# Two of four block sums of each square layer made by accumulating transfers on GpSimd's queue, with signs turned; the weights' check spread over one more tile

## The reference, cut to what matters

```
h = silu(x @ w1.T * w1_s) * (x @ w2.T * w2_s)
h = gelu(h @ h1_w.T * h1_s)          # square layer 0
h = gelu(h @ h2_w.T * h2_s)          # square layer 1
g = silu(h @ w3_w.T * w3_s)
```

## Time and profile before

| | us |
|---|---|
| median of 3 runs | 1295.23 (1295.19 to 1295.3) |
| profiled execution, its own time | 1296.77 |
| its span in the trace | 1295.0 |

### The profile page before, as it was taken

How to read it: one execution, slowest core, us unless ns; L and a number is a source line. 1 busy time by engine, 2 the same in 40 slices (tenths; PEclk the granted TensorE clock), 3 DMA queues, 4 the chain that set the end, 5 groups by cost and what they waited for, 6 DMA issues and landing times.

```text
span 1295.0 us, 16588 instructions
## 1 busy us (share of the span) xinstructions
PE 1284.7 (99%) x6066; PEld 1065.8 (82%) x6066; DVE 974.9 (75%) x1239; ACT 762.0 (59%) x1012; POOL 800.2 (62%) x804
## 2 busy tenths in 40 slices
PE   8999999999999999999999999999999999999997
PEld 7788888888888888888888888888888888888887
DVE  7888778778787777868777787777878777556675
ACT  4566655666556665565655656557565566555664
POOL 7964015999669995699947999388984890040000
PEclk9999999999999999999999999999999999999999
DMA  9698935455254541654416454265432644213441
GB/s 336 260 370 243 295 116 169 162 165 176 78 171 161 169 163 70 182 172 152 163 73 196 152 177 135 82 191 173 157 130 86 210 156 146 99 66 130 139 159 47
DMA packets 98199, 209.62 MB, mean 162 GB/s; under 512 B 14144, under 2 KB 17472, under 8 KB 97088
## 3 DMA queue, kind: packets, MB, share of 16 engines
q1 hardware_dynamic: 80176, 157.11, 36.2%
q0 software_dynamic: 17936, 51.39, 12.7%
HBM read 175.92 MB, written 38.83 MB: 166 GB/s over the span
## 4 chain that ended last, share of the span: by engine, by line
PE 98%; DVE 1%; ACT 0%; issue 0%; POOL 0%; POOLq 0%
PE ps L791 63%; PE ps L691 18%; PE ps L846 9%; PE ps L756 4%; PE ps L742 1%; PE ps L826 0%; PE ps L815 0%; PE ps L804 0%; PE ps L819 0%; PE ps L807 0%; PE ps L823 0%; PE ps L812 0%; PE ps L862 0%; DVE split L1330 0%; PE ps L680 0%; PE ps L880 0%
## 5 line engine op out<-in xcount | busy, mean ns | idle before, releaser
L791 PE MATMUL ps<-split,ring 128*128 128x512 f32 x3584 | 815.4, 389 | 0.0
L791 PEld LDWEIGHTS ps<-split,ring 128*128 128x128 f32 x3584 | 672.7, 188 | 139.7 <-DVE split L1324 0.4
L1324 DVE TENSOR_TENSOR split<-quad,split 128x1024 fp32r<-128x1024 f32 x224 | 290.4, 1305 | 143.3 <-ACT split L955 142.3
L955 ACT ACTIVATE split<-quad 128x1024 fp32r<-128x1024 f32 x224 | 231.5, 1052 | 42.1 <-PE ps L791 42.1
L691 PE MATMUL ps<-xT,w 128*128 128x512 f32 x1024 | 236.3, 391 | 1.0 <-ACT xT L1041 0.8
L691 PEld LDWEIGHTS ps<-xT,w 128*128 128x128 f32 x1024 | 190.9, 188 | 42.8 <-DVE quad L1318 2.0
L1000 ACT ACTIVATE quad<-quad,cols 128x512 f32<-128x512 f32 x192 | 136.5, 719 | 65.6 <-DVE quad L1355 38.0
L1347 DVE TENSOR_TENSOR quad<-quad 128x1024 f32<-128x1024 f32 x128 | 173.2, 1394 | 0.0
L537 POOL TENSOR_TENSOR ry<-ry,s 128x256 f32<-128x256 f32 x56 | 40.7, 759 | 200.7 <-issue 115.3
L938 ACT ACTIVATE rows<-ps,cols 128x512 f32<-128x512 f32 x128 | 87.2, 687 | 92.9 <-PE ps L691 47.2
L1318 DVE SCALAR_TENSOR_TENSOR quad<-ps,cols,rows 128x512 f32<-128x512 f32 x128 | 94.4, 745 | 47.4 <-ACT rows L938 30.7
(11 more groups left out here) (162 smaller groups left out, 1245.0 us busy)
## 6 DMA issues: line engine op xcount, KB each, us to landing
ring<-hs SPq DMA_DIRECT2D x428, 256.0 KB, 3.6
xin<-in_x SPq DMA_DIRECT2D x16, 512.0 KB, 4.2
s_h<-s SPq DMA_DIRECT2D x16, 512.0 KB, 4.5
seen<-in_h POOLq DMA_DIRECT2D x64, 128.0 KB, 2.9
ry<-in_x SPq DMA_DIRECT2D x15, 512.0 KB, 5.0
out<-ry SPq DMA_DIRECT2D x15, 512.0 KB, 2.6
z_h<-xin POOLq DMA_DIRECT2D x56, 128.0 KB, 3.8
xT<-z_h POOLq DMA_DIRECT2D x14, 512.0 KB, 6.5
```

What stands on the lines that cost most here:

```text
L791: mm = e.matmul(ps[:, 4 * (w % 2) + m, :], ring[n % RING][:, m * P:(m + 1) * P], slot[:, k, g, :], start=first and k == 0 and g == 0, stop ...
L955: e.activation(both(slots[i][:, :, 0, :], g), both(quad[at[t][L][name]], g), ACT.Identity).then_inc(hi, 1)
L1324: e.tensor_tensor(both(slots[i][:, :, 1, :], g), both(quad[at[t][L][FAST[w][1]]], g), both(slots[i][:, :, 0, :], g).bitcast(F32), ALU.subt ...
```

## The change

t3 and t4 of both layers are no longer made on DVE. `add_late` issues, on POOL's queue, transfers from SBUF to SBUF that add their source to their destination: t3 = b12 + b22 and t4 = t2 + b21, two transfers of 128 x 1024 numbers (512 KB) each. A sum by a transfer can only add, so signs are turned elsewhere: t1 and t2 become sums as well (`subtract` is now `add_up`), two of the four `fold_round` instructions change their operation, and two of the outputs' additions on DVE become subtractions. ACT's `high` waits for the transfer's semaphore (`late_sum`) where it waited for DVE's. The transfers stand on POOL's list behind `rows_in` and between groups of chunks of the check; in tile 0 they stand behind the last `fold_round`, among the ring's loads. The check takes 14 chunks a tile instead of 16, and the last 4 are done in tile 7.

```diff
-CHUNKS_A_TILE = 16
+CHUNKS_A_TILE = 14
...
         def n_sum(t, L, i, g):
-            return (2 * t + L) * 8 + 2 * i + g + 1
+            return (2 * t + L) * 4 + 2 * i + g + 1
...
-                e.tensor_tensor(a22, a21, a22, ALU.add).then_inc(folded, 1)
+                e.tensor_tensor(a22, a21, a22, ALU.subtract).then_inc(folded, 1)
...
-                e.tensor_tensor(a12, a12, a11, ALU.subtract).then_inc(folded, 1)
+                e.tensor_tensor(a12, a12, a11, ALU.add).then_inc(folded, 1)
...
+            def add_late(t, L, name):
+
+                src = {"t3": "b22", "t4": "b21"}[name]
+                for g in range(2):
+                    if name == "t3":
+                        on.wait_ge(block_sum, n_sum(t, L, 0, g))
+                        if L == 0:
+                            on.wait_ge(gated, n_gate(2 * t + 1, Q + 2 * g + 1))
+                        else:
+                            on.wait_ge(gelu["b22"], n_block(t, 0, 2 * g + 1))
+                    else:
+                        on.wait_ge(lo, n_split(t, L, 2, g))
...
+                    dst, src_ = both(quad[at[t][L][name]], g), both(quad[at[t][L][src]], g)
+                    e.dma_start(dst, src_, accum_op=ALU.add).then_inc(late_sum[name][g], 16)
...
-                    count_good(CHUNKS_A_TILE * (t - 1), CHUNKS_A_TILE * t)
+                begin = CHUNKS_A_TILE * (t - 1)
+                if t:
+                    parts = (begin, begin + 2, begin + 6, begin + 8, begin + CHUNKS_A_TILE) if t < END else (begin, begin + 4)
+                    add_late(t, 0, "t3")
+                    count_good(parts[0], parts[1])
+                    add_late(t, 0, "t4")
+                    if t < END:
+                        count_good(parts[1], parts[2])
+                    add_late(t, 1, "t3")
+                    if t < END:
+                        count_good(parts[2], parts[3])
+                    add_late(t, 1, "t4")
+                    if t < END:
+                        count_good(parts[3], parts[4])
                 if t == 0:
-                    for n in range(RING, 2 * NW * Q):
+                    n = RING
+                    for L, w, name in ((0, 0, "t3"), (0, 2, "t4"), (1, 0, "t3"), (1, 2, "t4")):
+                        while n < min((L * NW + w) * Q + RING, 2 * NW * Q):
+                            feed_raw(n)
+                            n += 1
+                        add_late(t, L, name)
+                    while n < 2 * NW * Q:
                         feed_raw(n)
+                        n += 1
                     e.dma_start(w3[:, :, :], w_kpm["w3"]).then_inc(d_w3, 16)
...
-                if name[0] == "t":
+                if name in ("t1", "t2"):
                     on.wait_ge(block_sum, n_sum(t, L, int(name[1]) - 1, g))
+                elif name in ("t3", "t4"):
+                    on.wait_ge(late_sum[name][g], 16 * (2 * t + L + 1))
...
-                e.tensor_tensor(dst, a, b, ALU.subtract).then_inc(block_sum, 1)
+                e.tensor_tensor(dst, a, b, ALU.add).then_inc(block_sum, 1)
...
-                    e.tensor_tensor(quad[t1][:, m, :], ps[:, Q + m, :], quad[t1][:, m, :], ALU.add).then_inc(c_sum["b22"], 1)
+                    e.tensor_tensor(quad[t1][:, m, :], ps[:, Q + m, :], quad[t1][:, m, :], ALU.subtract).then_inc(c_sum["b22"], 1)
...
-                                elif w == 0:
-                                    subtract(t, 0, 2, m - 2)
-                                elif (w == 2 if t == 0 else w == 1) and m >= 2:
-                                    subtract(t, 0, 3, m - 2)
```

More of the change, by code:

```diff
@@ L188, in build @@
         d_seen = [sem(f"d_seen{i}") for i in range(2)]
+        late_sum = {n: [sem(f"d_{n}{g}") for g in range(2)] for n in ("t3", "t4")}
         rows_turned, own_turned, own_dots = sem("rows_turned"), sem("own_turned"), sem("own_dots")
@@ L543, in add_y @@
                     e.tensor_tensor(res[:, b, :], res[:, b, :], yt[:, b, :], ALU.add).then_inc(pool_out, 1)
+            def add_late(t, L, name):
[9 more added lines that the diff above has]
+                        on.wait_ge(lo, n_split(t, L, 2, g))
+                        if L == 0:
+                            on.wait_ge(gated, n_gate(2 * t, Q + 2 * g + 1))
+                        else:
+                            on.wait_ge(gelu["b21"], n_block(t, 0, 2 * g + 1))
+                    dst, src_ = both(quad[at[t][L][name]], g), both(quad[at[t][L][src]], g)
+                    e.dma_start(dst, src_, accum_op=ALU.add).then_inc(late_sum[name][g], 16)
             chunks = [w_kpm[n][:, k, c:c + COUNT] for n in ("h1", "h2", "w1", "w2", "w3")
                       for k in range(w_kpm[n].shape[1]) for c in range(0, w_kpm[n].shape[2], COUNT)]
-            assert len(chunks) * COUNT * P == WEIGHTS and len(chunks) <= CHUNKS_A_TILE * (NT - 2)
+            assert len(chunks) * COUNT * P == WEIGHTS and len(chunks) <= CHUNKS_A_TILE * (NT - 2) + 4
             def count_good(first, last):
@@ L1331, in low_last, with add_up @@
                                 both(slots[i][:, :, 0, :], g).bitcast(F32), ALU.subtract).then_inc(last_lo, 1)
-            def subtract(t, L, i, g):
+            def add_up(t, L, i, g):
                 for name in SUMS[i][1:]:
@@ L1361, in product_out @@
                     on.wait_ge(u2_kept, n_block(t, L, m))
-                    e.tensor_tensor(quad[b11][:, m, :], here, quad[b11][:, m, :], ALU.add).then_inc(c_sum["b12"], 1)
+                    e.tensor_tensor(quad[b11][:, m, :], here, quad[b11][:, m, :], ALU.subtract).then_inc(c_sum["b12"], 1)
             def sums_of_proj():
@@ L1517, in _ @@
                     low(t, 0, 1, 1)
-                    subtract(t, 0, 0, 0)
-                    subtract(t, 0, 0, 1)
+                    add_up(t, 0, 0, 0)
+                    add_up(t, 0, 0, 1)
                 for L in range(2):
@@ L1533, in _ @@
                                     if t == 0:
-                                        subtract(t, 0, m, 0)
-                                        subtract(t, 0, m, 1)
+                                        add_up(t, 0, m, 0)
+                                        add_up(t, 0, m, 1)
                                     elif m == 0:
-                                        subtract(t, 0, 1, 0)
-                                        subtract(t, 0, 1, 1)
-                                elif w == 0:
-                                    subtract(t, 0, 2, m - 2)
-                                elif (w == 2 if t == 0 else w == 1) and m >= 2:
-                                    subtract(t, 0, 3, m - 2)
+                                        add_up(t, 0, 1, 0)
+                                        add_up(t, 0, 1, 1)
                                 elif w == NW - 1 and m >= 2:
-                                    subtract(t, 1, 0, m - 2)
+                                    add_up(t, 1, 0, m - 2)
                             elif w == 0 and m >= 2:
-                                subtract(t, 1, 1, m - 2)
-                            elif (w, m) in ((1, 2), (2, 2)):
-                                subtract(t, 1, 2, w - 1)
-                            elif (w, m) in ((2, 3), (3, 2)):
-                                subtract(t, 1, 3, w - 2)
+                                add_up(t, 1, 1, m - 2)
                             if 0 < t < END and L == 0 and w in (2, 3) and m >= 2:
```

## The result

| | before | after |
|---|---|---|
| median | 1295.26 | 1335.99 (1334.3 to 1336.26, 4 runs) |
| ratio after/before | | 1.0309 [1.0294, 1.0325] |
| span of the profiled execution | 1295.0 | 1332.4 |
| DVE busy | 974.9 | 895.4 |
| PE busy | 1284.7 | 1299.3 |

The change makes the kernel 3.1% slower, 40.7 us by the medians and 37.4 by the spans. 1306.5 was forecast, with a range up to 1318. The direction was right, the size was not.

What follows compares the result with a forecast made beforehand. PE was taken as the bound, so relieving DVE gains 0 us. The span of 1295.0 plus a 10.5 us stall in tile 0 plus 1.0 for PE's restart gave 1306.5 us, range 1300 to 1318.

Steps and rivals of the forecast that it cites:

- What bounds the kernel: PE bounds every tile and never waits inside; taking 89 us of block sums off DVE is worth 0 us.
- The spread check: Check at 14 chunks in tiles 1 to 6, four in tile 7: in time by 5 us, 0 us.
- Tile 0, POOL's list: t3 of layer 0 stands behind all eight folds; last fold store issued at 82.2 us, bounds 82.2 and 85.8.
- Tile 0, the landing: t3 lands at 95.0, product 4 begins at 97.4; PE idles 10.5 us, bounds 5.3 and 16.1.
- The clock: PE's slower restart after idling before product 4 of tile 0: 1.0 us, bounds 0 and 2.1.
- The step that failed: Tiles 1 to 7: sharing engines for 4 us delays ring pieces 2 to 4 us, inside their slack: 0 us.
- Rival 2: Ring starves in tiles 1 to 6 too, pieces landing after 9.3 to 10.6 us: 4 to 12 more; chance 0.14.
- Rivals 3 to 5: Add four times a copy, 1357 us (chance 0.05); not slower, 1295 to 1297.6 (0.07); faster, at most 1.2 us (0.02).

Runs made afterwards that it cites:

- x12: Changed kernel, but t3 of layer 0 in every tile and all of tile 0's sums made on DVE; 42 adding transfers left: 1296.45 us, ratio 1.0014.
- x1: Changed kernel, but both layer 0 sums of tile 0 made on DVE again: 1323.54 us, ratio 1.0224.
- x2: Changed kernel, but only tile 0's two layer 0 sums made by transfers, all others on DVE: 1312.61 us, ratio 1.0135.
- x3: Changed kernel with the same transfers only copying, not adding (output differs): 1311.36 us, ratio 1.0132.
- x9: Changed kernel plus 14 fp32 matmuls of zeros on PE before product 4 of tile 0: 1331.85 us, ratio 1.031.
- x5: Changed kernel, but only t3 of layer 0 in tiles 1 to 7 made by transfers, all other sums on DVE: 1309.67 us, ratio 1.0099.
- x10: Changed kernel, but only layer 1's sums made by transfers, in all tiles, layer 0's on DVE: 1300.94 us, ratio 1.0041.
- x8: Changed kernel with tile 0's layer 0 sums on DVE and, in tiles 1 to 6, a check chunk between a sum's two halves: 1314.98 us, ratio 1.0136.

## Why the prediction was right or wrong

**What bounds the kernel: right.** DVE lost 79.5 us of busy time (85 to 89 expected; 86.1 went with the sums, but `low` took 7.6 longer), and no variant gained from it. In x12 the sums move and PE's 101.56 stays.

**The spread check: right.** 0 us. Tile 7 is 101.57, and nothing waits for the count.

**Tile 0, POOL's list: the place right, the time partly luck.** The store was forecast for 82.2 and issued at 82.12. But of its three last tensor instructions two took 1.29 us, as forecast, and the first still 2.15, and an earlier one grew to 2.16. From the store of 59 us on the list became 2.7 us shorter and not 3.6; the other 1.0 came from the program's start, where everything, product 0 too, is about that much earlier. x1 and x2 confirm the place.

**Tile 0, the landing: a little short.** Product 4 was to begin at 97.4 and began at 98.78; the wait is 12.9 us for 10.5, inside the bounds of 5.3 and 16.1. Of these 2.4 us, 1.4 are the step "I take the middle of 93.0 and 97.0": t3 was there at 96.4, near the dear end. The other 1.0 is POOL's list, since PE wanted product 4 at 85.9 and not at 86.9. The Trainium skill's rule of half a copy's rate ("Collectives: The Full Stack", The bandwidth ceiling: the fold count and why AG ≠ RS ≠ AR) gave 12.5 us; the 2.1 times of engine time in x3 agrees with it. In x3, with the addition gone, only 2.1 us of the wait came back, since the fold's store ahead and the loads beside it stay.

**The clock: the term was too small.** "I take 1.0 here, bounds 0 and 2.1" measured 3.1, in x2 too (75.77 us for 320 matmuls), and 0.3 with PE kept busy in x9. The bound came from 28 small matmuls at the program's start. Here full-sized ones ran at the 1.2 GHz level for some 5 us. The Trainium skill's rule that the clock is at half rate again after idling ("TensorE: Matmul & The Clock Gate", Part 1: The HAM clock gate), which I had set beside a printed clock of 1.00, is what happened: 0.50 stands in the windows. The printed 1.00 was no reading: in the trace of before the first record of the clock begins at 5.3 us, and for the time ahead of it the page prints 1.00.

**The step that failed** is the last one on tiles 1 to 7: "A transfer that shares the engines for 4 us can add 2 to 4: inside. 0 us". It is worth 18.6 us in tiles 1 to 6; the same effect on the ring, which the prediction did not look for in tile 0's layer 1, costs 4.8 there, 23.4 together. By the spans 1306.5 was forecast and 1332.4 came, 25.9 more: 23.4 of it from the ring, 2.4 from tile 0's wait, 2.1 from the clock behind it, less the 1.7 at start and end, to within 0.3. The transfers do land in time for their own readers; that half of the step held. What failed is the neighbour. The pair holds the engines not for 4 but for 5.8 us (2 x 2.9), beside s's store and the load of xT, which were there already; and the ring does not get half of the engines meanwhile but every second packet, of small ones. Its group landed after 9.2 to 9.8 us for 4.3 to 5.3, where 8.6 were to be had.

**Rival 2** named this mechanism and the place, and gave it 9.3 to 10.6 us of landing, close to what came. Its price, 4 to 12, fell short twice: around each listed wait about as much again is lost, to hidden waits, long steps and the clock (x5: 9.2 us of waiting, 18.8 of loss), and it left out tile 0's layer 1 (x10). With both it would have read 1319 to 1335. I had spoken against it with 3.3 us of slack taken from a landing without this neighbour, and I never added the engine time asked for in that stretch.

**Rivals 3 to 5** are out. An addition costs 2.1 copies and not four; it was not free; and nothing was gained.

**Open.** Why t4 costs nothing alone, while in after some of the ring's waits lie beside t4: there they come only in tiles where t3 has been late before. Why x1's runs scatter over 8 us and what they lose beyond x5 and x10, and whether x8's halves help. Why the steps beside a late piece are 0.31 to 0.35 us long at a granted clock of 1.00. What decides whether the clock falls behind a short wait: it did behind 1.6 us in x5's tile 3, and did not behind 2.7 us in four pieces in x9's tile 0. No run separates these.

## What to carry to other kernels

Work taken off an engine that isn't the bound gains nothing, but the transfers that replace it are put into places where others were just in time: before moving a sum to a transfer, add up the engine time of all that is under way in the few microseconds around each just-in-time load, and count an addition at twice a copy. Where two queues meet, ask for the size of a packet on each, since the one with small packets loses in proportion; smaller packets of the background transfer help it, as long as their issues have room. Where pieces come late, don't take PE's listed waits for the loss: here the tiles grew by about twice their sum, so compare the length of a whole stretch of matmuls before and after.

## What the hardware showed that I had not expected

- Two queues on the same engines moved packets one for one: 91 to 91 with packets of 4 KB against 2 KB, 203 to 205 with 1 KB against 2 KB. The turns are nearly even, not exact. An adding packet of 4 KB took 0.327 us of one engine, a plain one 0.159, an adding one of 1 KB 0.10, the ring's 2 KB 0.084 to 0.098.
- An SBUF to SBUF transfer that adds 512 KB held the 16 engines for 2.9 us and landed after 8.2 us in the median; without the addition it was 1.35 us and 6.1.
- After 2.3 us of standing in two pieces, the granted clock was 0.54 and 0.61 in the next 4 us; after 12.9 us it was 0.50 to 0.59 for 6 us. With PE kept busy by zeros in that last stretch it stayed at 1.00. Most short waits had no such fall behind them: one in six tiles of after, three in six of x5. But each late piece cost more than PE's row of it says.
- The issue of one such transfer holds POOL for 0.94 us in the median (0.83 at least); the same transfer without the addition, in x3, for 0.54.
